# Flamingo block with sorted experts: rows sorted in five chunks of 4, 3, 3, 3 and 2 groups in place of six, tiles of one half, and a rearranged start

## What is computed

```python
ln = layernorm(layernorm(x), gamma_lat, beta_lat)         # latents, queries
kv = concat([layernorm(ctx, gamma_media, beta_media), ln]) @ Wkv + bkv
q  = (ln @ Wq + bq) * 128 ** -0.5                         # 8 heads of 128
x1 = x + tanh(g_xattn) * (softmax(q @ k.T) @ v @ Wo + bo)
p  = softmax(layernorm(x1) @ Wr + br);  top_p, top_i = top_k(p, 2)
h  = relu(layernorm(x1) @ W1[e] + b1[e])                  # 128 -> 256
y  = h @ W2[e] + b2[e]                                    # 256 -> 128
out = x1 + tanh(g_ffn) * (top_p[0] * y[top_i[0]] + top_p[1] * y[top_i[1]])
```

## Time and profile before

| | us |
|---|---|
| median of 3 runs | 812.92 |
| lowest, highest | 812.81, 813.12 |
| profiled execution, its own time | 810.86 |
| its span in the trace | 809.1 |

### The profile page before, as it was taken

One profiled execution on the slowest core, in us unless ns is written; L12 is line 12 of the kernel. 1 busy time (PEld: TensorE's weight loads), 2 busy tenths in 40 slices (PEclk: granted clock), 3 DMA queues, 4 the chain that ended last, 5 costly groups with the idle time before them and its releaser, 6 DMA issues.

```text
span 809.1 us, 17546 instructions
## 1 busy us (share of the span) xinstructions
PE 762.6 (94%) x5418; PEld 647.6 (80%) x5418; DVE 546.2 (68%) x1841; ACT 500.4 (62%) x1631; POOL 445.4 (55%) x454
## 2 busy tenths in 40 slices
PE   4899999998999999999999999999999999979887
PEld 4778777777888988778988878898877898968765
DVE  4637686685858568687758777776869556565445
ACT  2677677676766566766666666656667665555522
POOL 2234264636553544685655586665478566566662
PEclk9999999999999999999999999999999999999999
DMA  5845151532454542175764227574315556534522
GB/s 137 219 185 196 60 206 69 209 143 80 133 195 151 204 165 70 35 237 169 214 207 140 61 74 239 185 234 150 118 56 163 183 179 217 189 105 136 142 70 84
DMA packets 121551, 121.53 MB, mean 150 GB/s; under 512 B 14681, under 2 KB 95858, under 8 KB 121458
## 3 DMA queue, kind: packets, MB, share of 16 engines
q1 hardware_dynamic: 111890, 102.56, 38.8%
q0 software_dynamic: 7680, 15.74, 6.6%
q10 hardware_dynamic: 1888, 2.10, 0.9%
HBM read 36.34 MB, written 41.94 MB: 97 GB/s over the span
## 4 chain that ended last, share of the span: by engine, by line
PE 76%; DVE 7%; issue 6%; POOL 6%; ACT 3%; DMA 1%; ACTq 0%; SPq 0%; DVEq 0%; POOLq 0%
PE shared L1365 13%; PE batch L1303 11%; PE batch L1316 10%; PE hid_ps L1239 8%; PE xy_ps L1253 7%; PE batch L1311 6%; PE shared L1165 3%; PE shared L1167 3%; PE shared L1166 3%; PE batch L1253 2%; POOL probs L650 2%; PE xy_ps L1216 2%; ACT probs L716 2%; POOL yg L640 2%; PE batch L1293 2%
## 5 line engine op out<-in xcount | busy, mean ns | idle before, releaser
L650 POOL TENSOR_TENSOR probs<-probs,rsums 128x512 f32<-128x512 f32 x128 | 133.1, 1040 | 237.7 <-DVE rsums L1096 236.8
L716 ACT ACTIVATE probs<-batch,neg_max 128x128 f32<-128x128 f32 x512 | 180.8, 374 | 3.7 <-DVE neg_max L1100 3.7
L625 POOL DMA_INDIRECT sorted_x<-xn,row_of x120 | 124.7, 1039 | 33.6 <-issue 28.8
L797 ACT ACTIVATE qT<-shared,tb 128x512 f32<-128x512 f32 x128 | 87.3, 697 | 86.0 <-PE shared L1167 73.2
L1303 PE MATMUL batch<-kvT,qT 128*128 128x128 f32 x1024 | 136.3, 276 | 0.8 <-ACT qT L797 0.8
L1316 PE MATMUL batch<-pT_sb,kvn 128*128 128x512 f32 x256 | 133.2, 602 | 2.8 <-ACT pT_sb L724 2.7
L1303 PEld LDWEIGHTS batch<-kvT,qT 128*128 128x128 f32 x1024 | 125.2, 193 | 1.2 <-ACT qT L797 1.2
L1365 PE MATMUL shared<-M,oT 128*128 128x128 f32 x1024 | 125.4, 276 | 0.2
L1365 PEld LDWEIGHTS shared<-M,oT 128*128 128x128 f32 x1024 | 119.4, 192 | 1.4 <-issue 1.3
L716 ACT ACTIVATION_READ_ACCUMULATOR probs<-batch,neg_max 128x1 f32 x512 | 110.0, 215 | 0.0
L1096 DVE RECIPROCAL rsums<-sums 128x4 f32<-128x4 f32 x128 | 22.6, 177 | 123.7 <-ACT probs L716 115.3
(11 more groups left out here) (166 smaller groups left out, 1265.7 us busy)
## 6 DMA issues: line engine op xcount, KB each, us to landing
wt<-wall SPq DMA_DIRECT2D x128, 321.0 KB
sorted_x<-yg SPq DMA_DIRECT2D x36, 512.0 KB, 4.9
xt<-sorted_x SPq DMA_DIRECT2D x168, 64.0 KB
sorted_y<-y_sb SPq DMA_DIRECT2D x84, 128.0 KB
kv<-in_ctx_dram SPq DMA_DIRECT2D x16, 256.0 KB
kv<-in_x_dram SPq DMA_DIRECT2D x16, 256.0 KB
xres<-in_x_dram SPq DMA_DIRECT2D x32, 128.0 KB
out_dram<-x SPq DMA_DIRECT2D x16, 256.0 KB
```

Of the source, the lines that this page charges most:

```text
L625: nc.gpsimd.indirect_dma_start(xs[k % SETS][:, :], bass.IndirectOffsetOnAxis(ap=row_of[:, g, choice, c:c + 1], axis=0), xn[:, g % 2, c, :] ...
L650: nc.gpsimd.tensor_tensor(pv, pv, rsums[:, m % 2, :].unsqueeze(2).broadcast_to([P, 4, P]), ALU.mult).then_inc(probs_ready, 1)
L716: last = nc.scalar.activation(probs[:, m % 2, c * P:(c + 1) * P], batch_ps[m % BANKS][:, c * P:(c + 1) * P], ACT.Exp, bias=neg_max[:, m % ...
L797: nc.scalar.activation(qT[:, g % 2, :, number, :], sh[:, :].rearrange("p (b i) -> p b i", b=GB), ACT.Identity, bias=tb[:, number:number + ...
```

## The change

- **Chunks.** CHUNKS becomes (4, 3, 3, 3, 2). The halves become (39, 31, 31, 31, 23), the tiles (20, 16, 16, 16, 12), 80 in all. Tile slots are 51 to 70, 75 to 90, 99 to 114, 123 to 138 and 139 to 150. The room for an expert's rows grows from 1536 to 2048, so J, the halves that an expert can have, from 12 to 16, and the clears from 36 to 48 DMAs (slots 1 to 48). Dense slots stay 151 to 158. The last two sorted groups share a chunk: group 14's gathers are issued in slots 157 to 161, group 13 is added in slots 160 and 161, group 14 in 162; LAST goes from 160 to 164.
- **Halves.** PARTS says for each tile whether it has two halves or one. The last tile of each chunk has one, and its second half is left out on every engine and in its DMAs, so that 155 halves remain.
- **Homes.** The five DVE instructions for home move from the slot with s = 1 to the one with s = 4.
- **Start.** SP instead of ACT issues the second half of the weights. The constant every is written by ACT (a copy that is ACT's first instruction). The folded heads use four banks in place of two. DVE scales all keys first, without waiting for rstd, then shifts them all, and then keeps heads 0 to 3.

```diff
-CHUNKS = (3, 3, 3, 3, 2, 1)
+CHUNKS = (4, 3, 3, 3, 2)
...
+PARTS = tuple(min(2, HALVES[k] - 2 * t) for k in range(NCH) for t in range(TILES[k]))
...
+        fold_ps, FB = batch_ps, BANKS
...
-            for half in range(2):
-                if half == 1:
-                    act.wait_ge(got_kv, 32)
...
+            load_weights(act, 0)
+            act.wait_ge(const_step, 4)
+            nc.scalar.activation(every[:, :], ones_sq[:, :], ACT.Copy).then_inc(every_ready, 1)
...
                     sp.dma_start(Wr_f[:, :], Wr).then_inc(got_gates, 16)
+                    load_weights(sp, 1)
...
+                if n == FOLD_FROM:
+                    for k in range(4):
+                        scale_kv(0, k)
+                    for k in range(4):
+                        shift_kv(0, k)
...
+            def find_homes(n, s):
+
+                g = n // GB - 2
+                if s == HOMES and g in LAST_GROUP:
...
             def turn_tile(i):
-                pe.wait_ge(got_x[i % XB], 32 * (i // XB + 1))
+                pe.wait_ge(got_x[i % XB], 16 * halves_to(i, XB))
...
-                for a in range(2):
+                for a in range(PARTS[i]):
...
-                    fold = batch_ps[h % 2]
-                    if h >= 2:
-                        pe.wait_ge(w_lo, h - 1)
+                    fold = fold_ps[h % FB]
+                    wait(pe, w_lo, h - FB + 1)
```

## The result

| | us |
|---|---|
| before, median of 20 runs (lowest, highest) | 812.33 (810.53, 813.42) |
| after, median of 20 runs (lowest, highest) | 809.63 (806.80, 815.19) |
| ratio, 95% interval | 0.9969, 0.9956 to 0.9982 |
| profiled execution of after, its span | 809.19, 807.2 |

The change gains 2.7 us where 8.4 were forecast. The time lies inside the range given, but the forecast of how much is gained was wrong, and one term of its sum carries nearly all of that.

A forecast was written before the change was run, and what follows sets the result against it. PE's work was taken to bound the middle, latencies the start, list and end. Terms -9.3 - 1.2 - 1.8 - 1.0 + 4.9 = -8.4 us took 812.9 to 804.5, range 799.0 to 810.0.

The forecast's parts named there:

- The start: Start of the kernel: earlier cols and scaling keys before rstd gain 1.8 us, between 0.5 and 3.0.
- Middle halves, lists and homes: Before slot 131: 11 fewer halves gain 9.3 us; lists and homes, less the wider table, gain 1.2 with the last list.
- The price of a half: Tile slots: each half taken out saves 0.84 us, from octets with and without tiles; 1.00 as the other end.
- a list there costs nothing and moving homes gives nothing: Octets full of tiles: PE does not idle, so lists and homes there count 0; homes gain 1.3 in the tile-free octet.
- The tail of tiles: Slots 131 to 150: two single tiles gain 1.0 us, between 0 and 2.0.
- its list: Group 14's list in slot 129: shorter homes give back about 0.8 us, the wider table costs 0.45.
- The 0.8 that it expected back in slot 129: Slot 129: PE waited 0.80 us for DVE behind group 14's list; moving homes gives back about 0.8.
- The end: After the last dense hidden layer: late gathers and group 14's sum lose 4.9 us, 13.9 instead of 9.0.
- The slow case at slot 138: Third rival: the load at the new chunk border comes late, PE idles and its clock halves; 819.5 us, chance 0.07.
- The end eats more: Second rival: gathers land at 5.9 (2.9 more) and the start gains only 0.5; 808.7 us, chance 0.17.
- the clock was once halved: Sign for the slow rival: after idling PE got half its clock once, eight matmul records taking 1.77 against 1.13.
- the fourth rival: No measurable change: several terms at poor ends (halves 7.5, lists 0, start 0.5, tail 0, end 7.8); 812.7 us, chance 0.05.

The follow-up runs named there:

- the two repeats of after: The changed kernel run again unchanged beside the kernel before: 809.51 us, ratio 0.9972; and a third time on the fifth chip: 789.46 us, ratio 0.9922.
- full tiles: The changed kernel with all tiles given two halves again (160, the added five empty): 811.57 us, ratio 0.9988 against the kernel before.
- the repeat: The changed kernel unchanged, a third time, on the fifth chip, where the kernel before took 795.38: 789.46 us, ratio 0.9922.

## Why the prediction was right and wrong

**The start** was taken at 1.8. POOL's first scaling came at 33.23, 1.0 earlier than the 34.2 forecast, but the slot behind it gave 1.6 back (4.01 us between the first two scalings instead of 2.41), and at sequence 8 the gain is 1.2. In the two repeats of after the first scaling comes at 33.5 and 34.4, the distance is 2.41 again, and at sequence 8 the gain is 2.5 and 1.6. The term was right within what one execution shows.

**Middle halves, lists and homes.** Behind the start, 10.6 us are gained to the last scaling (9.7 and 10.6 in the repeats), where the terms made 9.3 for halves and 0.85 for homes less the wider table, 10.2; the sum is right. Its parts are less so. The price of a half was 0.84 and is 0.9 where it was measured. The slot of the list in slot 41 fell from the 6.93 of the earlier trace rows to 5.94 as forecast. The step that "a list there costs nothing and moving homes gives nothing" in octets with tiles failed: homes were worth 3.3 us ahead of the tail and not 1.3. The slot with a list grew by 1.3 in each full octet when homes stood in it, and the earlier trace rows, an average over eight slots, could not show that. With 3.3 for homes and 9.3 for halves the sum would be 12.2, more than the 10.6 measured, and the chunks without the other parts gained only 1.6 there; why the parts don't add up is open. So the sum is right in part by luck.

**The tail of tiles** is the step that failed: -1.0 forecast, and -0.4 for its list, against +4.7. It has two parts. Of the 4.7, 4.0 stand between the last scaling and slot 131 (18.11 us instead of 14.15); from there to slot 150 it is 2.3 more (moving the gathers alone brought 2.1 there in the kernel before), and the dense slots take 1.6 less. The 4.0 come from the plan of gathers, in which the new chunks put five into slots 128 and 129 instead of two: moving them away brought 4.7 us back there, cost 1.9 ahead of it, and was worth about 3 of the time. The prediction followed the gathers only at the end and never asked where the others had gone; it took their effect on the other engines in the tail at nothing, without a reason. The 0.8 that it expected back in slot 129, where the last list stands, is lost in the same wait. The other part is the sentence "1.7 us if PE were the limit; it is idle 12 of 73.8 us, so I take 1.0". On these chips PE alone doesn't set the tail: without its gathers it is 18 to 20 us shorter. Whether the two halves gave the 1.0 all the same isn't shown; with full tiles the tail was 106.0, against 105.9 and 104.9.

**The end** was right, nearly term by term. The chain of after, its last pieces:

```profile
791.24 0.94 POOL qT L664
...
798.49 2.46 DMA qT<-sorted_y,home
800.95 0.02 issue
800.97 1.15 DVE x L1105 x4
```

The fifth gather is issued 5.4 us after the last hidden layer (5.2 forecast), lands after 2.46 (3.0 taken), then DVE adds for 2.31, and 14.1 us pass in all (13.9 forecast, 9.0 before). By the Trainium skill, page "DMA: Bandwidth & Descriptors", section "Anatomy of one DMA — SWDGE (gpsimd) path", the landing was estimated at 2.15; the trace lies between the two.

**The rivals.** The slow case at slot 138 did not come about. "The end eats more", 808.7, is the nearest in time to 809.6 and wrong in its reason, so that this nearness is luck, as is the measured time's place inside the range. No rival had the gathers slow the tail. Three small points of the working: that the clock was once halved shows in 1.77 against the 0.89 of the earlier trace rows rather than against 1.13, the pieces of the end add up to 814.1 and not 814.0, and the halves' poor end of 7.5 in the fourth rival has no working. None of them changes the forecast.

**On the chips without the hold** the change gains 5.9 us (789.46 against 795.38), still less than 8.4. There the gathers don't slow the tail, the last dense hidden layer is done at 770.9, and POOL has the last word. The chain of the repeat:

```profile
777.57 3.38 DMA qT<-sorted_y,home
```

POOL issues without a pause until 778.5, the end takes 16.3 us instead of the 13.9 forecast (14.1 was expected of this run), and group 14's results are the last to arrive. No profile of the kernel before was taken there, so that its own end is not known.

**What stays open:** by what way POOL's gathers make PE's signals late on those chips. Shown are that moving the gathers moves the hold, that neither plain DMAs of the same size nor a POOL without them has it in slots 128 to 138, and that the same program on other chips has none. Not shown is whether an unbroken row is needed there or each gather costs its share, since the runs meant for that fell on chips without the hold. Nor is it shown whether the chip or the occasion makes the difference, or whether the hold needs the recording: every time on record is of an execution whose span was recorded, and where the hold is, records of signals are missing too (164 of 256 are there in the tail of after, 250 of 256 in that of the repeat on the fifth chip). One reading is made unlikely. By the Trainium skill, page "SBUF — State Buffer", section "SBUF: two separate sides", only VectorE and GpSimd share a port and ScalarE never waits for anyone. Here ACT was the first to stand idle (3.37 us), and for a signal of PE, so a fight for that port does not explain it.

## What to carry to other kernels

A change in the size of a stage shifts everything that is planned by counting from its end. Before such a change is priced, list where each moved step lands, the background ones too, and look at what stands in a row there; here five gathers in two slots cost 4 us, where the 11 halves ahead of the tail were priced at 9.3, and the best version that computes everything was the one that left the chunks alone (0.9883). Price work taken out of a stretch only after asking what sets that stretch, and keep the average of a stretch apart from its worst slot. And compare kernels on the same chip and the same occasion: a 17 us difference between chips looked like the success of an edit.

## What was not expected of the hardware

- While POOL issued indirect DMAs one behind the other (0.94 us and 0.30 between), ACT, DVE and PE were held up on three chips and in the result: PE done at 691.06 by its record, ACT released at 693.57, while the last gather of the row was issued (693.40 to 694.34). The 60 gathers of the tail made it 18 to 20 us longer there (103.6 and 105.9 against 85.6).
- The signals that came late were PE's alone: 47 of 74 over 0.3 us behind the recorded end in the tail of after, none of 90 of ACT, DVE and POOL.
- On the other two chips the same program shows none of it, even with 53 gathers in one row: 0.03 us in the same place, the tail 84.2 us, and the kernel before 795 us instead of 812.
- Where PE idled more it was granted less clock: 0.92 over the tail of after (17.5 us idle), 0.97 in that of before (13.7), 1.00 in the one without the hold (4.7).
